# One block for all stages: the first feed-forward prepared inside the convolution's last group

## The reference

```python
x = x + tanh(g_xattn[0]) * L0_xattn(ctx, ctx, layernorm(x), ssm_kernel, D, 8)  # kv outer products per head, causal convolution over 256, times q
x = x + tanh(g_ffn[0])   * L0_ffn(layernorm(x), ...)   # shared 1024-wide SiLU-gated part + top 2 of 8 experts
x = x + tanh(g_xattn[1]) * L1_xattn(layernorm(x), ctx, ctx)  # 16 heads of 16, causal inside 128 positions
x = x + tanh(g_ffn[1])   * L1_ffn(layernorm(x), ...)   # shared 256-wide relu^2 part + top 6 of 32 experts, grouped routing
return x
```

## Time and profile before

| | |
|---|---|
| median of 3 runs | 952.78 us (952.51 to 954.13) |
| profiled execution | 953.02 us, its span 950.9 us |
| TensorE (PE) | 911.2 us busy, 96% of the span |
| VectorE (DVE) | 606.5 us, 64% |
| ScalarE (ACT) | 545.1 us, 57% |
| GpSimd (POOL) | 200.6 us, 21% |
| granted TensorE clock, mean | 0.991 |

### The profile page before, as it was taken

How to read it: one execution, slowest core, us unless ns; L and a number is a source line. 1 busy time by engine, 2 the same in 40 slices (tenths; PEclk the granted TensorE clock), 3 DMA queues, 4 the chain that set the end, 5 groups by cost and what they waited for, 6 DMA issues and landing times.

```text
span 950.9 us, 13975 instructions
## 1 busy us (share of the span) xinstructions
PE 911.2 (96%) x4730; PEld 725.0 (76%) x4748; DVE 606.5 (64%) x1397; ACT 545.1 (57%) x946; POOL 200.6 (21%) x171
## 2 busy tenths in 40 slices
PE   6799889999999999989999999999999999999998
PEld 5799767877788888856666667778788888888886
DVE  6678655456563556568888866656855466556554
ACT  3222043433453334448889676777777877777774
POOL 5899400000000001227777540000000000000000
PEclk8899999999999999999999999999999999999999
DMA  8100030233211152114544405344444344444443
GB/s 303 59 1 2 1 116 18 77 108 112 85 48 51 61 191 85 37 37 163 169 175 157 156 15 165 127 133 136 137 151 145 92 133 138 148 146 134 150 124 103
DMA packets 57957, 104.36 MB, mean 110 GB/s; under 512 B 7296, under 2 KB 13824, under 8 KB 57504
## 3 DMA queue, kind: packets, MB, share of 16 engines
q1 hardware_dynamic: 57168, 103.34, 33.6%
q10 hardware_dynamic: 720, 0.14, 0.1%
HBM read 101.03 MB, written 2.42 MB: 109 GB/s over the span
## 4 chain that ended last, share of the span: by engine, by line
PE 47%; DVE 3%; ACT 2%; DMA 1%; issue 1%; POOL 0%; SPq 0%; DVEq 0%; ACTq 0%; POOLq 0%
PE bank L1125 19%; PE bank L1092 18%; PE bank L1393 2%; PE bank L1404 2%; PE bank L1385 1%; PE bank L1386 1%; DMA k_blocks_sb<-in_k_blk 1%; PE bank L1413 1%; PE bank L1381 1%; DVE shifted_scores L1583 1%; PE bank L534 1%; DMA Gf<-gates 1%; PE bank L778 0%; PE bank L760 0%; DVE max L1577 0%
## 5 line engine op out<-in xcount | busy, mean ns | idle before, releaser
L1092 PE MATMUL bank<-xhf,whif 128*128 128x512 f32 x528 | 211.5, 401 | 2.2 <-ACT rf L856 1.5
L1092 PE MATMUL bank<-xlf,whif 128*128 128x512 f32 x528 | 207.7, 393 | 0.0
L1092 PE MATMUL bank<-xhf,wlof 128*128 128x512 f32 x528 | 207.7, 393 | 0.0
L875 ACT ACTIVATE yhif<-yf 128x512 fp32r<-128x512 f32 x200 | 124.1, 622 | 83.2 <-DVE yf L962 82.5
L976 DVE TENSOR_TENSOR yf<-yf,Gf 128x512 f32<-128x512 f32 x124 | 85.8, 692 | 122.8 <-ACT yf L864 120.3
L1125 PE MATMUL bank<-yhif,whif 128*128 128x512 f32 x400 | 159.2, 398 | 3.4 <-DVE ylof L739 2.9
L1125 PE MATMUL bank<-yhif,wlof 128*128 128x512 f32 x400 | 157.4, 394 | 0.0
L1125 PE MATMUL bank<-ylof,whif 128*128 128x512 f32 x400 | 156.5, 391 | 0.0
L739 DVE TENSOR_TENSOR ylof<-yf,yhif 128x512 fp32r<-128x512 f32 x196 | 134.4, 687 | 30.0 <-ACT yhif L875 29.7
L858 ACT ACTIVATE rf<-bank 128x512 f32<-128x512 f32 x136 | 81.1, 596 | 83.4 <-PE bank L1092 83.3
L1092 PEld LDWEIGHTS bank<-xhf,whif 128*128 128x128 f32 x528 | 99.0, 188 | 25.4 <-ACT rf L856 1.9
(11 more groups left out here) (136 smaller groups left out, 1213.2 us busy)
## 6 DMA issues: line engine op xcount, KB each, us to landing
Gf<-gates SPq DMA_DIRECT2D x156, 256.0 KB, 3.7
wrawf<-in_wu SPq DMA_DIRECT2D x68, 256.0 KB, 2.6
k_blocks_sb<-in_k_blk SPq DMA_DIRECT2D x64, 256.0 KB, 4.2
wrawf<-in_wu SPq DMA_DIRECT2D x32, 384.0 KB, 3.0
v_slot<-in_v_rows SPq DMA_DIRECT2D x16, 256.0 KB, 2.6
ctx_windows<-in_ctx_win SPq DMA_DIRECT2D x3, 1024.0 KB, 10.8
toeplitz<-in_kpad SPq DMA_DIRECT2D x4, 512.0 KB, 9.0
X<-in_x SPq DMA_DIRECT2D x4, 512.0 KB, 9.2
```

Source lines behind the costliest of these rows:

```text
L875: act.activation(yhi[:, K % S, :], y[:, K % S, :], ACT.Copy).then_inc(s_yh, 1)
L1092: last = pe.matmul(o, w_[:, Nu % S, wc], x_[:, c, xs], start=(m == 0), stop=(m == 5))
```

## The change

All stages go into one block; the three barriers but the last are gone, and semaphores order what they ordered.

- In the convolution's last group TensorE gets, behind its steps, `transposed` for blocks 0 to 7 of `f0` (r = 1 to 4), `logits_t` (r = 5, 6) and `logits` (r = 6, 7). ScalarE makes the normalized rows now (`normed_row`, with bias and scale, in place of VectorE's `normed`), and GpSimd makes a `shifts` for them. `x_lo`, `w_lo` and `logits_copy` stand on VectorE behind `weigh` of the same steps.
- The first four weight loads of `f0` are issued on the convolution's queue, behind a wait for the pair products of the first three groups (their windows lie where the weights go).
- The last four `reduce` come behind `h_prod(0)` (two) and behind `h_prod(1)` (two), their `residual` on VectorE in units 0 and 1. `keep_clock` stays only at the kernel's start.
- `sigmoid(0)` comes behind unit 1, the routing in units 2 to 6 (before 0 to 4), `gates_t` in units 7 and 9 (before 6 and 8).
- The two feed-forwards share their weight, `y`, `r`, gate and token buffers; the attention's `shifted_scores` and `probs_t` are now `y` and `r`; `gated_y` works in place.
- The first two `scores` come before the last `o_prod` of `f0`, and the load of the Exp table before the last two `out_scaled`. Attention's `out_turned` waits for all four `out_scaled`.

The core of the diff (the rest moves the stage functions and renames buffers):

```diff
@@ convolution, all engines @@
+                sp.wait_ge(s_kv, 4 * (NG - 1))
+                sp.wait_ge(s_sq, 4 * (NG - 1))
+                for Nu in range(S):
+                    f0.weights(sp, Nu)
...
                     if q == 12:
                         deviations(pool, "f0", 0)
+                        shifts(pool, "f0", 0)
...
+                f0.router_hi(act)
+                for m in range(2):
+                    for j in range(BPB):
+                        f0.normed_row(act, m, j)
+                    if m == 0:
+                        act.wait_ge(s_kv, 4 * (NG - 1))
+                        f0.w_hi(act, 0)
+                for m in range(2):
+                    for c in range(2):
+                        f0.x_hi(act, m, c, x_bank)
+                f0.w_hi(act, 1)
+                f0.logits_t_copy(act, 0, x_bank)
+                f0.logits_t_copy(act, 1, bk(6))
...
+                    if b in (NB - BPB, NB - BPB + 1):
+                        pe.wait_ge(f0.s_lgc, 2)
...
+                        if g == NG - 1:
+                            if r == 1:
+                                pe.wait_ge(s_qx, 2 * NG)
+                            if 2 <= r <= 5:
+                                pe.wait_ge(f0.s_l, r - 1)
+                            if 1 <= r <= 4:
+                                f0.transposed(pe, (r - 1) // 2, (r - 1) % 2, x_bank)
+                            if r == 5:
+                                pe.wait_ge(f0.s_rw, 2)
+                                f0.logits_t(pe, 0, x_bank)
+                            if r == 6:
+                                pe.wait_ge(s_xd, NB - BPB)
+                                f0.logits_t(pe, 1, bk(6))
+                                f0.logits(pe, 0, x_bank)
+                            if r == 7:
+                                pe.wait_ge(f0.s_lc, 2)
+                                f0.logits(pe, 1, bk(6))
-                    for j in range(BPB):
-                        reduce(NB - BPB + j)
...
+                            if r == 0:
+                                f0.constants(dve)
+                                f0.router_lo(dve)
+                            if 1 <= r <= 4:
+                                f0.x_lo(dve, (r - 1) // 2, (r - 1) % 2, x_bank)
+                            if r == 5:
+                                dve.wait_ge(s_kv, NQ)
+                                dve.wait_ge(s_sq, NQ)
+                                f0.w_lo(dve, 0)
+                            if r == 6:
+                                f0.w_lo(dve, 1)
+                                f0.logits_copy(dve, 0, x_bank)
+                            if r == 7:
+                                f0.logits_copy(dve, 1, bk(6))
@@ feed-forward @@
-            GATES_T = (6, 8, KP_ + 1, KP_ + 3) if gated else (3, 3, KP_ - 14, KP_ - 8)
+            GATES_T = (7, 9, KP_ + 1, KP_ + 3) if gated else (3, 3, KP_ - 14, KP_ - 8)
-            ROUTED0, ROUTE0_STEP = (4, 2)
+            ROUTE0, ROUTED0, ROUTE0_STEP = 2, 6, 2
...
+                        if K == ROUTE0 - 1:
+                            sigmoid(0)
...
+                if not final:
+                    tail.exp_table(act)
                 for s in range(2):
                     out_scaled(1, s)
...
                         dve.wait_ge(s_gl[j % S], gates_loaded(j))
-                        dve.tensor_tensor(t[:, K % S, :], r[:, K % S, :], G[:, j % S, :], ALU.mult).then_inc(s_gu, 1)
+                        dve.wait_ge(s_yh, K - S + 1)
+                        dve.tensor_tensor(mem.y[:, K % S, :], mem.r[:, K % S, :], mem.G[:, j % S, :], ALU.mult).then_inc(s_gu, 1)
...
+                        else:
+                            pe.wait_ge(ctx.s_z, 8 * BPB - 1 + K)
                         h_half(K, 0).then_inc(s_hg, 1)
...
-                    keep_clock(pe, bk(0), 10)
...
+                    for j in range(2):
+                        ctx.reduce(NB - BPB + j)
...
+                    if gated and K == 0:
+                        for j in range(2, 4):
+                            ctx.reduce(NB - BPB + j)
+                    if not final and K == NK - 1:
+                        pe.wait_ge(s_ac, NK)
+                        tail.scores(pe, 0)
+                        pe.wait_ge(s_yd, NK)
+                        tail.scores(pe, 1)
                     o_prod(K)
@@ attention @@
-                    scores(pe, 0)
-                    scores(pe, 1)
+                pe.wait_ge(f0.s_os, 4)
                 f0.out_turned(pe, 1, 0, 0, o_bank)
```

More of the change, by code:

```diff
@@ L156, in build, with context_stage @@
+        def context_stage():
+            A = Stage()
+            pa = ExitStack()
             NG, NQ = NB // BPB, NB
```

2205 lines of the change are left out of this document (1095 added, 1110 removed).

## The result

The changed kernel takes 936.21 us (median of 4 runs, 935.47 to 936.94), the kernel before beside it 953.45 (4 runs); the ratio is 0.9833, with a 95% interval of 0.9818 to 0.9848. The forecast was 944.6, in a range of 941.5 to 948.5: the sign was right, the gain is 17.2 us and not 8.4. The profiled execution has a span of 933.6 us, 17.3 less than before.

A forecast was written before the change was run, and what follows sets the result against it. TensorE, busy 911.2 of 950.9 us, was taken as the bound, leaving the seams between stages. Savings of 7.5 - 0.75 + 1.4 = 8.15 us from 953.02, with the median 0.24 lower, gave 944.6, range 941.5 to 948.5.

The forecast's parts named there:

- The rest costs nothing in the sum: Remaining edits (in-place gated_y, shared attention and second feed-forward buffers, f1 weight loads) were to cost no time.
- there is nothing to win: First feed-forward's long stretch: 269.95 us of matmuls in 270 us, six-matmul groups of 1.39 us, so no gain there.
- something in the new buffers: Rival: an unseen effect in the new buffers or the attention's pace, to either side; chance 0.05.
- Seam 1: Convolution to first feed-forward, up to output unit 0's end: 15.9 us taken out, 5.24 + 3.0 put in, 7.5 saved.
- The stall: Group 3, before the first f0 transposes: TensorE waits 5.24 us for normalized rows that hang on GpSimd's power.
- the slow spell: Half-rate clock after the idle in group 3: 3.0 us lost, chosen as nearest the 5.52 idle; lower end 1.4.
- clock back early: Rival: clock recovers early or never falls in group 3, up to 1.6 us more saved, 943.0; within clock variants' 0.70.
- No new bound in group 3: TensorE stays the slower engine, 6.8 against VectorE's 6.4 us per two quads; opposing rival 948.2, chance 0.11.
- No stall: Rival: rows before the first f0 transposes are ready before TensorE arrives, 8.2 us more saved, 936.4; chance 0.05.
- Unit 10: Transposes of block 2 wait there for the copy of the second gates: 0.75 us lost, bounds 0 and 1.2.
- Seam 2: First feed-forward to attention: out_turned starts 1.4 us earlier, with the Exp table load hidden; bounds 0 and 1.8.
- The table load: Exp load before the last scalings, forecast hidden without a drain; rival with drain 1.4 us more, 946.0, chance 0.06.

The follow-up runs named there:

- e10: Kernel before the change, with unused bytes around x_hi and x_lo so they agree with weights and y modulo 256: 940.88 us, ratio 0.9893.
- e3: Kernel before the change, with x_hi and x_lo placed last in each feed-forward's memory: 942.18 us, ratio 0.9900.
- e13: Changed kernel with x_hi_last and x_lo_last moved on by 192 bytes, as far off modulo 256 as x_first: 944.06 us, ratio 0.9920.
- e4: Changed kernel with f0's first power and shift moved on GpSimd ahead of the pair products of quad 15: 928.73 us, ratio 0.9765.
- e12: Changed kernel with 22 extra matmuls filling TensorE's stall before the first transposes, to keep the clock up: 935.87 us, ratio 0.9840.
- e9: Changed kernel with unused bytes around x_first (64 ahead, 192 behind), so x, weights and y agree modulo 256: 931.59 us, ratio 0.9794.
- e18: As e9, with buffers TensorE never reads (w_raw, activated, y, gate_rows) moved on by 64 bytes: 931.51 us, ratio 0.9780.
- e11: As e9, with w_hi and w_lo moved on by 64 bytes, out of agreement with x and y: 946.95 us, ratio 0.9948.

## Why the prediction was wrong

**The step that failed** is the one headed "The rest costs nothing in the sum": "Shared buffers for attention and second feed-forward have the slots and the owners they had", and with it the reading of the earlier trace rows as a stretch in which "there is nothing to win". I took the 1.39 us of six matmuls for the price of the work, and it held a price of where the buffers lie. The change moved `x_last` to the weights' remainder modulo 256 bytes and made blocks 8 to 15 faster: 32 units of `f0` by 0.10 (3.2 us) and 68 of `f1` by 0.05 (3.4 us), against 68 others in `f1` slower by 0.01 (0.7). Nothing in the diff aims at it. e10 and e3 show that the place does it without the change, e13 that without the place the changed kernel takes 944.06. The chance of 0.05 for "something in the new buffers" was the right case; its size was far outside the range.

**Seam 1** gave 9.27, not 7.5. The stall was right (5.16 for 5.24). The term that was mis-sized for the profiled execution is the slow spell: 3.0 forecast. It ended about as after the idle of 3.10; e4 finds 0.9 for all that the stall drags behind it, and e12 finds that a full clock alone would save some 0.15. The rival "clock back early" was the one that happened there, with its price nearly right (1.6 against 1.8 more). But it did not happen for good: seven of thirteen profiles with this very stall have the long spell, and with e9's the seam gives 7.7, close to the forecast. The choice by the nearest idle had no ground: the same idle is followed by either spell, and the 3.10 of the earlier trace rows, short in the trace that I read, is followed by the long one in e3 and e10.

**No new bound in group 3**, as forecast: no wait for `x_lo` stands in the changed kernel's list. e12 shows how near it is (0.97 at full clock, 1.5 forecast).

**No stall.** That rival was put at 8.2 more, and e4 measures 7.5. Its 936.4 is nearly the measured 936.21, by chance: the stall stands in the profile, and other terms made the time. It was named against the queue that GpSimd had, which was right for the changed kernel; it was also the best next edit.

**Unit 10** was 0.59 for 0.75. **Seam 2**: from the last `o_prod` to `out_turned` 1.64 less (412.48 to 415.48 before, 400.55 to 401.91 after), the attention behind it 0.35 less (133.27 to 132.92 up to the first `h_prod` of `f1`), and the `scores` moved ahead cost `f0` about 0.5: 1.5 for the forecast 1.4. The table load had no drain behind it: it ends at 399.19 and the next activation starts at 399.20, so the Trainium skill's rule (ScalarE: Activation LUTs, What ACT_TABLE_LOAD costs), by which some 1380 ns would follow, is not seen here either.

**The sum.** 0.57 + 9.27 - 0.6 + 1.5 + 3.2 + 3.44 = 17.4, against 17.3 between the spans. The forecast had 8.15, so 9.2 are unforeseen: 6.6 in the feed-forwards, 1.8 in seam 1, 0.6 scatter of the start, the rest small. Without the feed-forwards' faster matmuls the forecast would have been off by 0.5 as e13 has it (7.85 more than the changed kernel), and by 2.5 by the periods (5.9). Two errors partly cancel in e13: the spell was priced too high, and in e13 blocks 0 to 15 of `f1` run at 2.78, slightly slower than before.

None of the three signs that the prediction names for being wrong came: the stall was there, no waits for `x_lo`, and the attention 0.35 shorter. The part that failed had no sign of its own.

**Still open.** Why the two reads of TensorE get in each other's way unless they agree modulo 256 bytes: the runs show that they do, by how much for offsets of 64, 96, 128 and 192, and that no other engine takes part. Which circuit does it they can't show. No run has `y` alone off, or matmuls of another shape or type. What decides between the short and the long spell of the clock is open too. Of the 2.3 that e9's profile lacks from unit 0's end on against the periods, only the 0.8 in waits for `y_lo` are followed.

## What to carry to other kernels

When a change moves buffers, compare the time of one repeated piece of work before and after, and in both halves of a loop, not only the seams that it is meant for: 5 ns in a matmul came to 6 to 8 us here, against 9.3 for the seam of the first barrier. Where the clock falls, look at more than one execution before you price the spell. In a kernel bound by 512-column matmuls of 32-bit operands, let the weights and the moving operands begin at the same remainder modulo 256 bytes; a few unused bytes gave 1.1% here. And where a queue waits for a short instruction of a slow engine, see first whether that instruction's inputs were there earlier: here they were there 5.95 us before it ran.

## What the runs showed of the hardware

- The step of back-to-back 128x512 matmuls on fp32r operands, at a granted clock of 1.00, was 226.7 ns with all operands in agreement modulo 256 bytes, 231 to 233 ns with `x` off, and 233.3 ns with the weights off from all. The matmuls on `y` slow with those on `x` when only `x` is off (230 to 231 ns). The Trainium skill (TensorE: Matmul & The Clock Gate, Wait — 56ns, not 53.3ns?) gives N / 2.4 GHz and about 2.5 ns more, 215.7 ns for 512 columns; no stretch here came to that, and the page has no term for a place.
- The Trainium skill (SBUF — State Buffer, SBUF: two separate sides) says that TensorE never waits on another engine's accesses. e18 agrees: other engines' buffers at another remainder left the step at 226.7 ns. e11 shows a slowdown among TensorE's own reads (233.3 ns), which that rule doesn't cover.
- A stall of 5.16 us was followed by about 3 us of work at the lower clock in six profiles (after: 96.88 to 99.7) and by about 6 us in seven (e9: 96.51 to 102.6). After 5.52 us in group 0 it was 6 us, and after 3.10 us it was 2.9 in the kernel before and 6.0 in e10 (111.52 to 117.5), the same code there: neither the length of the idle nor the work behind it said how long the clock stays low.
